# A wait of GpSimd's gathers on VectorE's products of hats in a deformable sampler

## The chip, the cores and the metric

The kernel runs on one core of a Trainium2 chip. The metric is the device time of one execution in microseconds, as the median of several runs. Profiles come from one further execution that the hardware profiler recorded.

## What is computed

Four layers follow one another on eight images of 64 channels and 32 by 32 pixels: a wavelet layer with sparse attention, a layer of convolutions and "adder" convolutions, a layer of quantised convolutions, and a modulated deformable convolution. The change lies in the code of the last two, which the kernel calls the sampler. What matters there of the reference:

```python
def deform_sample(x, py, px):              # x: (8, 64, 32, 32), two groups of 32 channels
    y0, x0 = jnp.floor(py), jnp.floor(px)
    fy, fx = py - y0, px - x0
    ...
    val = corner(y0i, x0i, (1 - fy) * (1 - fx)) + corner(y0i, x0i + 1, (1 - fy) * fx) \
        + corner(y0i + 1, x0i, fy * (1 - fx)) + corner(y0i + 1, x0i + 1, fy * fx)
    return val.reshape(Bb, DG, Cg, K, Hh, Ww)
off_out = conv2d(x, off_w) + off_b[None, :, None, None]
mask = jax.nn.sigmoid(off_out[:, 2 * DG * K:]).reshape(Bb, DG, K, Hh, Ww)
g = deform_sample(x, py, px) * mask[:, :, None]
out = jnp.einsum('odck,bdckhw->bohw', wr, g)
```

For each pixel, each of the two channel groups and each of the nine taps, four neighbouring pixels at a computed place are read and weighed.

## The kernel before, in words

The eight images lie in two halves of four; one "image" of the sampler is a pair, one of each half, on 128 partitions. There are NB = 4 such images and 16 steps in each (STEPS), so 64 steps (NT).

Seven of the nine taps are done by **gathers**. GpSimd (L1959 to L1975) issues, for each step, GK = 14 indirect DMAs; each fetches for 128 pixels one row of 128 floats, the four neighbours of 32 channels, from a table in HBM. They go into one of four buffers (RING = 4, the tile `sampler_G`), so the gathers of step `th` wait for the semaphore `used` to tell that VectorE is done with step `th - 4` (L1970). At an image's first step they also wait for the indices (`indexed`) and for the table (`stored`).

The other two taps are done **densely**: a pixel's weight on each row and each column is a hat function, and VectorE multiplies hats in y with hats in x (the *products of hats*, `mix`, L2055 to L2065; two parts of 128 x 2048 each, after each of which it raises `mixed`). So `mixed` stands at 2 * (n + 1) when step n is done.

In each step the engines do this, each in this order:

- VectorE: `sample(n)` (L2027 to L2039) waits for the 14 gathers of the step (`arrived`), multiplies them with their weights (L2032), adds the four neighbours (L2036), raises `val` and then `used`; then a piece of the next image's preparation (`next_stage`); then `mix(n)`, which waits for ScalarE's hats (`hy`), PE's spread hats in x (`hx_ps`) and PE's use of the products of the step before (`added`).
- PE: `turn_values(n)` transposes the sampled values (L2156); `contract(n - 1)` multiplies the products of hats with the image (L2195); a piece of the next image's preparation, a convolution (L1744) in ten of an image's sixteen steps; `spread_y(n + 1)` and `spread_x(n + 1)` (L2139, L2148), the latter after `mixed` tells that the products of step n are done; `deform(n - 2)`.
- ScalarE: copies the transposed values (L2239) and the dense values (L2268) out of PSUM, does its piece of preparation, and makes the hats of step n + 1 (L2260, L2262).

The preparation of the next image has twelve pieces (STAGES): two pieces of quantising, convolutions, and at last the offsets, from which VectorE makes the next image's gather indices (L1852 to L1872) and weights. PE does piece i in step i, VectorE and ScalarE in step i + 1. The last image has no next one.

The order on each engine is the order of the code; nothing reorders it. All waits are on semaphores.

Of the kernel before, what the change touches and what calls it, by code (L numbers as in the profile page):

```python
# [41 lines left out]
GK = DG * NTAP  # L42
# [150 lines left out]
def program(nc, A, C, out):  # L193
# [3 lines left out]
    with outer:  # L197
# [1462 lines left out]
        def sampler(st, sb, sem):  # L1660
# [50 lines left out]
            sig, x4_ps, x4, s4_ps, hxm, py_ps, hx_ps, hy, mixed, added, v_sb = (  # L1711
                sem(n) for n in ("sig", "x4_ps", "x4", "s4_ps", "hxm", "py_ps", "hx_ps", "hy", "mixed", "added", "v_sb"))
# [245 lines left out]
            with nc.Block() as blk:  # L1958
                @blk.gpsimd  # L1959
                def _(g):  # L1960
                    g.memset(AP[:, :, :], 0.0)
                    g.memset(WB[2][:, :, :], 0.0)
                    g.memset(zeros, 0.0)
                    g.drain().then_inc(cleared, 1)
                    for th in range(NB * STEPS):
                        b, step = th // STEPS, th % STEPS
                        if step == 0:
                            g.wait_ge(indexed, b + 1)
                            g.wait_ge(stored[b], 16 * NSTORE)
                        if th >= RING:  # L1970
                            g.wait_ge(used, th - RING + 1)
                        for k in range(GK):
                            g.indirect_dma_start(G[th % RING][:, k, :], None, tables[b],  # L1973
                                                 bass.IndirectOffsetOnAxis(ap=IDX[:, b % 2, step, k:k + 1], axis=0))\
                             .then_inc(arrived[th % RING], 16)  # L1975
# [134 lines left out]
                def _(t):  # L2110
                    def prepare_x(g):

                        b, k, ti, _, _ = unit(4 * g)
                        if g:
                            t.wait_ge(hxm, g)
                        if g >= 4 and g % 2 == 0:
                            t.wait_ge(e_sb, g // 2 - 1)
                        for e in range(4):
                            mm = t.matmul(MISC[32 * e:32 * e + 32, :], column(channel(e // DG, e % DG, ti) + 1, 32),
                                          half(OFF[:, b % 2], k), start=True, stop=True)  # L2120
                        mm.then_inc(x4_ps, 1)

                    def prepare_mask(g):

                        b, k, ti, _, _ = unit(4 * g)
                        t.wait_ge(sig, b + 1)
                        t.wait_ge(x4, g + 1)
                        for e in range(4):
                            ch = 64 * (e // DG) + 2 * DG * TAPS + (e % DG) * TAPS + NTAP + ti
                            mm = t.matmul(MISC[32 * e:32 * e + 32, :], column(ch, 32), half(SIG[:, b % 2], k),  # L2130
                                          start=True, stop=True)
                        mm.then_inc(s4_ps, 1)
# [193 lines left out]
```

## Time and profile before

| what | value |
|---|---|
| time, median of 3 runs (lowest to highest) | 4012.67 us (4010.67 to 4012.89) |
| span of the profiled execution | 4500.8 us |
| PE busy | 3405.0 us, 76% |
| VectorE (DVE) busy | 3169.4 us, 70% |
| ScalarE (ACT) busy | 2843.2 us, 63% |
| GpSimd (POOL) busy | 907.3 us, 20% |
| software DMA (the gathers) | 28672 packets, 58.78 MB |

The profiled execution's own time is known by its span alone, from the first to the last instruction. It is 488 us longer than the median of the timed runs. Busy times count an engine's instructions without its waits. PE's matmul ends are modelled, so a matmul can end later than its record says; what waits for it shows that. "remote" in a row is a wait whose end the profile could not put down to a known instruction.

### The profile page before, as it was taken

What the parts mean: (1) busy time and instruction counts of PE and PEld (TensorE: products, weight loads), DVE (VectorE), ACT (ScalarE), POOL (GpSimd) and SP (SyncE); (2) the same over time, 40 slices, a digit from 0 to 9 for tenths busy, and PEclk for the clock granted to TensorE, in tenths of its full rate; (3) what the DMA queues carried; (4) which work ended last, traced back from release to release, by engine and by line L of the source; (5) the groups of instructions that cost most, each with busy time, mean ns of one, the idle gap of its engine ahead of it and who ended that gap; (6) DMA issues with size and microseconds to landing.
All of it is one profiled execution on the core that took longest, in us unless ns stands there. A gap on an engine that the chain in (4) does not pass through costs nothing. (4 is left out here: it accounts for less than half of the span.)

```text
span 4500.8 us, 58636 instructions
## 1 busy us (share of the span) xinstructions
PE 3405.0 (76%) x22186; PEld 1347.4 (30%) x22186; DVE 3169.4 (70%) x3652; ACT 2843.2 (63%) x2698; POOL 907.3 (20%) x974
## 2 busy tenths in 40 slices
PE   3777559999999999999999998447556655674445
PEld 2454333233333333333334343112112212221111
DVE  5999768999999984999999994234435444444445
ACT  1444326999999994999999992234434444443444
POOL 2000010000000000000000000445554554545452
PEclk7656569999999999999999998757767777776667
DMA  2200000000000000000000000211211111121110
GB/s 43 89 1 1 1 3 1 1 1 1 1 1 2 2 1 1 1 1 1 1 1 2 2 1 13 52 34 38 54 41 38 47 46 33 43 54 39 39 41 21
DMA packets 117631, 89.65 MB, mean 20 GB/s; under 512 B 96496, under 2 KB 98576, under 8 KB 117340
## 3 DMA queue, kind: packets, MB, share of 16 engines
q0 software_dynamic: 28672, 58.78, 4.7%
q1 hardware_dynamic: 87036, 26.32, 2.6%
q8 instruction: 197, 3.23, 0.3%
q10 hardware_dynamic: 1632, 0.56, 0.1%
q14 instruction: 94, 0.77, 0.1%
HBM read 65.61 MB, written 19.96 MB: 19 GB/s over the span
## 5 line engine op out<-in xcount | busy, mean ns | idle before, releaser
L1556 ACT ACTIVATE adder_layer_Z<-adder_layer_CP,AN 128x2048 f32 x984 | 1873.3, 2013 | 33.4 <-PE PS L1517 32.6
L1517 PE MATMUL PS<-adder_layer_Z,c_adder_out 128*32 128x512 f32 x16896 | 1845.0, 593 | 57.9 <-ACT adder_layer_Z L1556 33.1
L1602 DVE TENSOR_SCALAR adder_layer_Z<-adder_layer_CP,AW 128x2048 f32 x1128 | 1369.9, 1281 | 45.5 <-PE PS L1517 31.5
L1517 PEld LDWEIGHTS PS<-adder_layer_Z,c_adder_out 128*32 128x32 f32 x16896 | 649.6, 110 | 1253.0 <-issue 1176.1
L1973 POOL DMA_INDIRECT sampler_G<-neighbours,sampler_IDX x896 | 849.6, 948 | 834.9 <-DVEq L2039 436.9
L2260 ACT ACTIVATE sampler_HY<-PS,G_hat 128x512 f32<-128x512 f32 x512 | 309.0, 686 | 319.6 <-PE PS L2139 119.6
L1609 DVE SCALAR_TENSOR_TENSOR adder_layer_Z<-adder_layer_CP,AW,adder_layer_Z 128x1024 f32<-128x1024 f32 x384 | 476.4, 1282 | 35.6 <-issue 35.6
L2148 PE MATMUL PS<-sampler_HXM,G_spread 32*128 32x512 f32 x128 | 99.1, 864 | 387.4 <-DVEq L2065 341.9
L2063 DVE TENSOR_TENSOR P<-sampler_HY,PS 128x2048 f32<-128x2048 f32 x64 | 146.4, 2287 | 338.9 <-remote 255.3
L2262 ACT ACTIVATE sampler_HY<-sampler_HY 128x2048 f32<-128x2048 f32 x128 | 244.6, 1911 | 8.7
L1474 POOL MEMSET XP<- 128x4624 f32 x1 | 4.0, 3952 | 1046.4 <-PE PS L1533 1046.4
L1469 POOL MEMSET adder_layer_CP<- 128x4624 f32 x2 | 7.9, 3954 | 1020.3 <-POOLq L1464 1020.2
L2036 DVE TENSOR_REDUCE sampler_VAL<-sampler_G 128x448 f32<-128x1792 f32 x64 | 208.9, 3265 | 5.8 <-issue 0.9
L1744 PE MATMUL PS<-XP,WB 128*128 128x512 f32 x288 | 154.2, 685 | 76.3 <-ACT sampler_HT L1799 52.2
L2063 DVE TENSOR_TENSOR RAW<-sampler_HY,PS 128x2048 f32<-128x2048 f32 x64 | 146.4, 2287 | 87.7 <-remote 65.1
L2024 DVE TENSOR_TENSOR sampler_HXM<-P,PS 128x512 f32<-128x512 f32 x16 | 11.0, 689 | 274.5 <-remote 169.6
L2148 PEld LDWEIGHTS PS<-sampler_HXM,G_spread 32*128 32x128 f32 x128 | 24.8, 241 | 444.9 <-issue 441.7
L2032 DVE TENSOR_TENSOR sampler_G<-sampler_G,PS 128x1792 f32<-128x1792 f32 x64 | 129.3, 2021 | 40.3 <-DMA sampler_G<-neighbours,sampler_IDX 28.7
L2268 ACT ACTIVATE sampler_VD<-PS 128x512 f32<-128x512 f32 x32 | 19.0, 593 | 209.8 <-remote 177.4
L2239 ACT ACTIVATE sampler_VT<-PS 128x384 f32<-128x384 f32 x64 | 31.1, 486 | 184.8 <-remote 145.1
L811 DVE MAX8 top_k_best<-top_k_WK 128x8 f32<-128x256 f32 x384 | 135.1, 415 | 10.3 <-issue 0.5
L699 PE MATMUL PS<-VT,top_k_PT 128*128 128x9 f32 x512 | 102.6, 339 | 50.8 <-ACT top_k_PT L764 50.8
(376 smaller groups left out, 3018.8 us busy)
## 6 DMA issues: line engine op xcount, KB each, us to landing
sampler_G<-neighbours,sampler_IDX POOLq DMA_INDIRECT x896
neighbours<-top_k_zero SPq DMA_DIRECT2D x16, 578.0 KB, 7.2
neighbours<-sampler_HT SPq DMA_DIRECT2D x256, 32.0 KB, 1.7
X<-in_x SPq DMA_DIRECT2D x8, 256.0 KB, 6.3
out<-X SPq DMA_DIRECT2D x8, 256.0 KB
P<-in_L_conv_conv_w SPq DMA_DIRECT2D x4, 144.0 KB
P<-in_L_conv_add_w SPq DMA_DIRECT2D x4, 144.0 KB
RAW<-in_L_conv_w SPq DMA_DIRECT2D x4, 144.0 KB
```

Source lines behind the costliest of these rows:

```text
L811: v.max(best[:, g % 2, u, 8 * r + 1:8 * r + 9], WK[:, u, :])
L1517: mm = t.matmul(PS[32 * j:32 * j + 32, k, :], K["adder_out"][:, 32 * i:32 * i + 32], Z[:, r % SLOTS, j, c:c + BANK], start=False, stop=Fal ...
L1556: op = a.activation(z(r, j), seen(ch, ty, tx), ACT.Relu, bias=ANf[:, weight(ty, tx, j, i)])
L1602: op = v.tensor_scalar(z(r, j), seen(ch, ty, taps[0]), AWf[:, weight(ty, taps[0], j, i)], 0.0, ALU.subtract, ALU.max)
L1609: op = v.scalar_tensor_tensor(out=z(r, j)[:, b], in0=seen(ch, ty, tx)[:, b], scalar=AWf[:, weight(ty, tx, j, i)], in1=z(r, j)[:, b], op0=A ...
L1744: mm = t.matmul(pre(k), w[:, tap, :], src[:, y:y + 16, x:x + W], start=(tap == 0), stop=(last and tap == TAPS - 1))
L1973: g.indirect_dma_start(G[th % RING][:, k, :], None, tables[b], bass.IndirectOffsetOnAxis(ap=IDX[:, b % 2, step, k:k + 1], axis=0))\
L2032: v.tensor_tensor(g3, g3, WP.unsqueeze(2).broadcast_to([128, GK * 4, CG]), ALU.mult)
L2036: v.tensor_reduce(VAL[:, th % 2, :, :], gt[:, :, :].rearrange("p k (q c) -> p k c q", q=4), AX.X, ALU.add)
L2063: v.tensor_tensor(M[part][:, :, :], HY[:, part], HXB.unsqueeze(1).broadcast_to([128, HATS, BANK]), ALU.mult)
L2260: a.activation(HY[:, part, j, :], PYB, ACT.Abs, bias=GR["hat"][:, c:c + 1])
L2262: a.activation(HY[:, part].rearrange("p c f -> p (c f)"), HY[:, part].rearrange("p c f -> p (c f)"), ACT.Relu, scale=-1.0, bias=1.0)\
```

## The change

In GpSimd's loop over the 14 gathers of a step, a wait is put ahead of the eighth, from step 2 on: until `mixed` stands at 2 * (th - 1), that is, until both products of hats of step th - 2 are done.

```diff
                         for k in range(GK):
+                            if th >= 2 and k == GK // 2:
+                                g.wait_ge(mixed, 2 * (th - 1))
                             g.indirect_dma_start(G[th % RING][:, k, :], None, tables[b],
                                                  bass.IndirectOffsetOnAxis(ap=IDX[:, b % 2, step, k:k + 1], axis=0))\
                              .then_inc(arrived[th % RING], 16)
```

GpSimd's instructions of the sampler, from the first gather on, before (the four buffers are `sampler_G0` to `sampler_G3`, the first image's table is `neighbours0`):

```order
L1973 DMA sampler_G0<-neighbours0,sampler_IDX 128x128 [waits sampler_stored0,sampler_indexed]
L1973 DMA sampler_G0<-neighbours0,sampler_IDX 128x128 x13
L1973 DMA sampler_G1<-neighbours0,sampler_IDX 128x128 x14
L1973 DMA sampler_G2<-neighbours0,sampler_IDX 128x128 x14
L1973 DMA sampler_G3<-neighbours0,sampler_IDX 128x128 x14
L1973 DMA sampler_G0<-neighbours0,sampler_IDX 128x128 [waits sampler_used]
L1973 DMA sampler_G0<-neighbours0,sampler_IDX 128x128 x13
```

The same place of GpSimd's queue after the change:

```order
L1975 DMA sampler_G0<-neighbours0,sampler_IDX 128x128 [waits sampler_stored0,sampler_indexed]
L1975 DMA sampler_G0<-neighbours0,sampler_IDX 128x128 x13
L1975 DMA sampler_G1<-neighbours0,sampler_IDX 128x128 x14
L1975 DMA sampler_G2<-neighbours0,sampler_IDX 128x128 x7
L1975 DMA sampler_G2<-neighbours0,sampler_IDX 128x128 [waits sampler_mixed]
L1975 DMA sampler_G2<-neighbours0,sampler_IDX 128x128 x6
L1975 DMA sampler_G3<-neighbours0,sampler_IDX 128x128 x7
L1975 DMA sampler_G3<-neighbours0,sampler_IDX 128x128 [waits sampler_mixed]
L1975 DMA sampler_G3<-neighbours0,sampler_IDX 128x128 x6
L1975 DMA sampler_G0<-neighbours0,sampler_IDX 128x128 [waits sampler_used]
L1975 DMA sampler_G0<-neighbours0,sampler_IDX 128x128 x6
L1975 DMA sampler_G0<-neighbours0,sampler_IDX 128x128 [waits sampler_mixed]
```

No instruction moved and no gather was added; from the third step on, the eighth gather carries a wait. The other engines' queues read as before but for line numbers, which are two higher from L1973 on.

## Rows read from the trace of the kernel before

**Rows 1.** Table of stretches: from:to, length, busy us (instructions) of each engine, PE's clock, DMA share, GB/s.
```profile
0.00:540.00 540.00, 345.10 (x1303) 233.13 (x1304) 442.34 (x1409) 212.57 (x637) 35.41 (x67) 0.63 0.10 28
540.00:2700.00 2160.00, 2027.01 (x17426) 742.64 (x17427) 1950.17 (x1724) 1907.97 (x1050) 16.08 (x7) 0.97 0.01 1
...
2854.40:4500.80 1646.40, 910.40 (x2990) 321.40 (x2990) 715.82 (x418) 685.03 (x967) 849.58 (x896) 0.71 0.16 41
```

**Rows 2.** Timeline of GpSimd, first and last gather: start, duration, instruction, [idle before].
```profile
2854.41 1.16 POOL L1973 DMA_INDIRECT sampler_G<-neighbours,sampler_IDX  x1 [99.47 <-DMA neighbours<-sampler_HT]
...
4438.52 0.94 POOL L1973 DMA_INDIRECT sampler_G<-neighbours,sampler_IDX  x1 [0.30 <-issue]
```

**Rows 3.** Groups of the sampler's stretch: busy us, mean ns, idle before, who ended it.
```profile
L1973 POOL DMA_INDIRECT sampler_G<-neighbours,sampler_IDX x896 | 849.6, 948 | 834.9 <-DVEq L2039 436.9 <-issue 265.9 <-DMA neighbours<-sampler_HT 99.5
```

**Rows 4.** Waits of the sampler's stretch: total us, times, longest.
```profile
DVE P L2063 <- remote: 255.3, 15, 26.1
```

**Rows 5.** Timeline of two steps, GpSimd, VectorE, PE and ScalarE, in part.
```profile
3541.16 0.94 POOL L1973 DMA_INDIRECT sampler_G<-neighbours,sampler_IDX  x1 [15.70 <-DVEq L2039]
...
3548.49 2.02 DVE L2032 TENSOR_TENSOR sampler_G<-sampler_G,PS 128x1792 f32<-128x1792 f32 x1 [0.19 <-issue]
...
3553.97 0.66 PE L2156 MATMUL PS<-c_ident,sampler_VAL 128*128 128x128 f32 x4 [2.24 <-DVEq L2038]
...
3557.41 0.95 POOL L1973 DMA_INDIRECT sampler_G<-neighbours,sampler_IDX  x1 [0.31 <-issue]
3558.66 0.94 POOL L1973 DMA_INDIRECT sampler_G<-neighbours,sampler_IDX  x1 [0.30 <-issue]
...
3564.47 0.49 ACT L2239 ACTIVATE sampler_VT<-PS 128x384 f32<-128x384 f32 x1 [7.51 <-remote]
...
3574.92 0.94 POOL L1973 DMA_INDIRECT sampler_G<-neighbours,sampler_IDX  x1 [0.30 <-issue]
3579.97 2.29 DVE L2063 TENSOR_TENSOR P<-sampler_HY,PS 128x2048 f32<-128x2048 f32 x1 [26.08 <-remote]
...
3590.64 0.95 POOL L1973 DMA_INDIRECT sampler_G<-neighbours,sampler_IDX  x1 [14.77 <-DVEq L2039]
```

**Rows 6.** Timeline, step 1: its last gather and VectorE's first use of it.
```profile
2888.41 0.95 POOL L1973 DMA_INDIRECT sampler_G<-neighbours,sampler_IDX  x1 [0.30 <-issue]
...
2891.02 2.02 DVE L2032 TENSOR_TENSOR sampler_G<-sampler_G,PS 128x1792 f32<-128x1792 f32 x1 [7.45 <-DMA sampler_G<-neighbours,sampler_IDX]
```

**Rows 7.** Timeline of VectorE, step 62 and the start of the last, after the last gather.
```profile
4460.87 2.02 DVE L2032 TENSOR_TENSOR sampler_G<-sampler_G,PS 128x1792 f32<-128x1792 f32 x1 [0.19 <-issue]
4462.97 3.27 DVE L2036 TENSOR_REDUCE sampler_VAL<-sampler_G 128x448 f32<-128x1792 f32 x1
4468.46 2.29 DVE L2063 TENSOR_TENSOR P<-sampler_HY,PS 128x2048 f32<-128x2048 f32 x1 [2.22 <-PE PS L2195]
4470.94 2.29 DVE L2063 TENSOR_TENSOR RAW<-sampler_HY,PS 128x2048 f32<-128x2048 f32 x1 [0.19 <-issue]
4473.41 2.02 DVE L2032 TENSOR_TENSOR sampler_G<-sampler_G,PS 128x1792 f32<-128x1792 f32 x1 [0.19 <-issue]
```

**Rows 8.** Table of stretches: a plain step, then two convolutions of 18 matmul records each.
```profile
4455.92:4468.46 12.54, 9.35 (x38) 3.32 (x34) 9.87 (x4) 10.02 (x14) 0.00 (x0) 0.73 0.00 1
3443.75:3451.74 7.99, 7.99 (x23) 3.67 (x20) 7.30 (x5) 1.27 (x2) 5.92 (x7) 1.00 0.20 58
3583.48:3594.29 10.81, 10.81 (x19) 4.48 (x19) 6.49 (x3) 0.00 (x0) 2.84 (x3) 0.74 0.44 74
```

**Rows 9.** Timeline of VectorE in step 44, which prepares the fourth image's indices.
```profile
4039.67 3.23 DVE L2036 TENSOR_REDUCE sampler_VAL<-sampler_G 128x448 f32<-128x1792 f32 x1
...
4052.47 0.46 DVE L1852 TENSOR_SCALAR sampler_pos<-sampler_T 128x224 f32<-128x224 f32 x2 [9.58 <-ACTq L1806]
...
4060.43 2.29 DVE L2063 TENSOR_TENSOR P<-sampler_HY,PS 128x2048 f32<-128x2048 f32 x1 [0.21 <-issue]
```

## The prediction

> **What bounds the kernel now.** I began with the page and the table of stretches. The program's first 540 us are a sorting and attention stage, up to 2700 us come the adder layers, and the sampler, which the change touches, issues its first gather at 2854.41 us [rows 1, 2]. In that last stretch of 1646.4 us no engine is full: PE is busy 910.40, GpSimd 849.58, VectorE 715.82 and ScalarE 685.03 us [rows 1]. By shares alone nothing there is a bound; the order in time has to tell.
>
> The list of groups and the waits say who waits: GpSimd's 896 gathers stood 834.9 us idle, 436.9 us of it for VectorE's release of a ring buffer; VectorE in turn stood 255.3 us before its products of hats for something the profile cannot name [rows 3, 4]. The timeline of one pair of steps shows how the two hang together [rows 5]. GpSimd starts at 3541.16, released by the sampling of some step n, and issues 28 gathers, for steps n + 4 and n + 5, every 1.25 us without a gap up to 3575.86. VectorE samples step n + 1 from 3548.49, and then stands 26.08 us, up to 3579.97, four microseconds after the burst. ScalarE too stands 7.51 us for a PE result whose matmuls have ended at 3554.63 by the record. From this burst to the next, at 3590.64, it is 49.5 us for two steps; that pattern, a short step and a long one, fills the stretch.
>
> **But this is not what the timed runs do.** The profiled execution spans 4500.8 us, the timed median is 4012.67 us: 488 us less. Where can they be? Up to 540 us VectorE is busy 442.34 of 540 us; in the adder layers PE is busy 2027.01 of 2160 us; both together leave 231 us of idle time on their fullest engines [rows 1]. So most of the 488 us must go in the sampler, where the nameless stalls are. A floor says how far: first gather at 2854.41 [rows 2], 896 gathers [rows 3] at 1.25 us [rows 5], which is 1120 us, and after the last gather's end 1.7 us of landing (the first steps, where VectorE waited for data: gather ended 2889.36, sampling began 2891.02 [rows 6]) and 27.4 us from the last sampling at 4473.41 to the end of the span [rows 1, 7]; the profiled run issued its last gather at 4438.52 [rows 2], long before that end. Sum 2854.4 + 1120 + 1.7 + 27.4 = 4003.5 us. The timed median lies 9 us above that. So I read the timed kernel as **bound by GpSimd's issue rate in the sampler**, 14 x 1.25 = 17.5 us a step, with almost no pause, and the stalls of the profile as belonging mostly to the profiled execution. A step without stage work needs 12.5 us of the others (sampling at 4460.87, the next at 4473.41 [rows 7]), so they can follow.
>
> The Trainium skill ("NOTIFIC — the notification-queue block", 7.1 Overflow: three behaviours, one of which stalls the engine) says that the block that writes trace records always holds back an engine inside itself rather than lose a record. No row here shows that this happened; it only makes the reading above less strange, and no number hangs on it.
>
> **The change, part by part.** It adds 62 waits (steps 2 to 63) to GpSimd, each ahead of the eighth gather; nothing is removed or moved. Queued behind a wait stand the seven gathers of the half and all later steps; VectorE's sampling waits for them. No other engine's queue changes.
>
> - *A wait that finds its count reached* costs nothing that I can see: the gather at 3558.66 carries the wait for a released buffer and starts 0.30 us after the one before, like those without a wait [rows 5]. 62 x 0 = 0. Upward the bound is one semaphore trip; I take 0.
> - *Does it find it reached?* Call G the end of the last gather of step m, with GpSimd never pausing. Sampling starts at G + 1.7 [rows 6]; from there to the end of the second product is 12.4 us (4460.87 to 4473.23 [rows 7]), so step m is mixed at G + 14.0. The eighth gather of step m + 2 is due at G + 0.30 + 17.5 + 8.75 = G + 26.5. **Slack 12.5 us**: no wait in a plain step. The old rule alone (buffer released at G + 1.7 + 5.4 = G + 7.1, first gather of m + 4 due at G + 52.8) had 45.7 us. The change takes 33 us of lookahead away, which costs nothing unless the others fall behind by over 12.5 us.
> - *Steps with stage work.* The step that prepares the next image's indices (three of them) is the latest. In the row, VectorE's reduction ends at 4042.90 and the product begins at 4060.43, 17.5 us against 2.2 us in a plain step (4466.24 to 4468.46) [rows 7, 9]. 15.3 us more than a plain step is 2.8 us over the slack. Of these 9.58 us are a wait for ScalarE, which was late in that row; with ScalarE less than 3 us earlier there is none. Three times 0 to 2.8 us: 0 to 8.4 us; I take 3, nearer the low end, since part of that lateness is the profile's.
> - *The first steps of the sampler*, where the ring is empty and convolutions of the next image begin: 0 to 5 us, an estimate by the same slack with one late convolution (10.81 instead of 7.99 us [rows 8]) and VectorE's stage work; I take 1.
> - *The data's way.* The second half, 7 x 1.25 + 1.7 = 10.5 us after its release, lands before VectorE asks for it, one plain step of 12.5 us after the products it waited for. So even where the wait does hold GpSimd, sampling of that same step is not late by itself; the lost gather time shows one step later.
>
> Sum: 4012.67 + 0 + 3 + 1 = 4017 us, +0.1%. Ends of these terms: +0 to +13 us. In the profiled execution GpSimd ran three steps ahead of the sampling [rows 5], so there the waits will be real and long; its span can move either way, and the time doesn't rest on it.
>
> **The rivals.**
> 1. *The lost lookahead costs: slower.* In eight steps in a row of an image PE also convolves. A plain step costs it 9.35 us, a convolution 7.99 us at a granted clock of 1.00 and 10.81 us in a stretch at 0.74 [rows 8]: 17.3 or 20.2 us against GpSimd's 17.5. At 20.2 the others fall 2.7 us behind per step, 21 us in eight steps; the old rule's 45.7 us swallow that, the new rule's 12.5 don't: 8.8 us lost, with the index step 11.6, in three images 35 us, so 4048 us. It decides from the point at which PE's convolution step passes GpSimd's by 1.6 us (12.5 over 8). For it: the two numbers are close and [rows 8] have both. Against it: with no stalls PE would be nearly always busy in these steps and, as in the row at clock 1.00, at the upper of its two levels, 2.4 GHz.
> 2. *The stalls are in the timed runs too, and shorter bursts relieve them: faster.* In the profile a pair of steps costs 49.5 us, of which 26.08 us are a stall that ends with the burst [rows 5]. Held at the half step GpSimd can issue at most up to the next unmet count, and then the others are let go. But the total can't fall under GpSimd's own 1120 us: 4003.5 us if the timed runs reach the sampler when the profiled one does, less by as much as they reach it earlier. Of the 231 us idle before it I take 10, so 3993 us. Against it: the timed time leaves 9 us, and a wait can't make the issuer faster.
> The Trainium skill ("Perfetto Trace Analysis", What "DMA-bound" means) would call issue the bound only where the issuer's track is solid with DMA slices. GpSimd's is at 52% here (849.58 of 1646.40 us [rows 1]), so by that rule rival 2's premise holds in the profile. Inside a burst it is solid, and the floor above is why I give that less weight.
> 3. *The wait is always reached:* 4012.7 us. It is the low end of the forecast and counts with it.
>
> **How the numbers follow.** Forecast with rival 3: 0.57. Rival 1: 0.28, between 4021 and 4050. Rival 2: 0.15, mostly between 3975 and 4004; it would gain in weight if the 1.25 us of a gather were partly the recording's, which no row can tell. About 0.2%, 8 us, is what a measurement of this kernel can tell from no change. Predicted 4017 us. The range of 3990 to 4046 us leaves out about half of rival 2 below and a quarter of rival 1 above. Faster 0.15, same 0.57, slower 0.28.
>
> **What would show it.** Right: the same time to a few us. In the profile of the changed kernel GpSimd's gaps of 0.30 us stay, most of its idle time is now ended by VectorE's drain after the products instead of its release after sampling, and gathers run about one step ahead of the sampling instead of three. Wrong: VectorE waiting often for arrived data would show that the 10.5 us don't fit; a timed gain over 9 us would show that the floor, and so my reading of the timed runs, is wrong.

## The result, and the profile after

The changed kernel takes **4017.45 us** (median of 20 runs, 4014.21 to 4021.52) where the kernel before takes 4013.05 (median of 20 runs, 4009.39 to 4015.54): 4.4 us more by the medians. The ratio over all runs is 1.0014, 95% interval 1.0008 to 1.0020, which is 3.2 to 8.0 us. It is a small loss, clear of zero, within the 0.2% for which the prediction said "same", and 0.45 us from the predicted time.

The page of the changed kernel begins with its span and the busy time of each engine, and its chain of work gives a share of the span to each engine:

```profile
span 4018.0 us, 58636 instructions
...
PE 3323.6 (83%) x22186; PEld 1330.0 (33%) x22186; DVE 3170.5 (79%) x3652; ACT 2840.5 (71%) x2698; POOL 908.6 (23%) x974
...
POOL 17%; issue 6%; PE 4%; DVE 2%; ACT 1%; SPq 1%; ACTq 0%; DMA 0%; DVEq 0%; POOLq 0%
```

The span lies right at the timed median, 483 us under the span of the profile of before, and GpSimd with its issue gaps (23% together) is the largest part of the chain. The engines did the same work as before; the stalls of [rows 3 to 5] are gone. The groups of instructions say it line by line (busy us, mean ns | idle before them, and what ended most of it):

```profile
L1975 POOL DMA_INDIRECT sampler_G<-neighbours,sampler_IDX x896 | 851.0, 950 | 379.7 <-issue 271.9
...
L2034 DVE TENSOR_TENSOR sampler_G<-sampler_G,PS 128x1792 f32<-128x1792 f32 x64 | 129.4, 2021 | 163.5 <-DMA sampler_G<-neighbours,sampler_IDX 159.0
...
L2065 DVE TENSOR_TENSOR P<-sampler_HY,PS 128x2048 f32<-128x2048 f32 x64 | 146.4, 2288 | 98.0 <-PE PS L2197 91.1
```

L1975 is the line of [rows 3]: its idle time fell from 834.9 to 379.7 us, and of that 271.9 are the 0.30 us gaps of issue. L2065 is the line of [rows 4]: no wait of it is put down to "remote" any more. VectorE now waits for gathered data (159.0 us), so the others follow GpSimd, not the reverse. The waits of the changed kernel from 2800 us to the end, GpSimd's alone (total us, times, longest), show the price of the new wait:

```profile
POOL sampler_G L1975 <- issue: 271.9, 892, 0.3
POOL sampler_G L1975 <- DMA neighbours<-sampler_HT: 100.2, 1, 100.2
POOL sampler_G L1975 <- DVEq L2067: 7.6, 3, 4.4
```

Of the 62 added waits, 59 found their count reached; three held GpSimd, 7.6 us in all. These are the three, in the timeline of GpSimd (start, duration, instruction, [idle before]):

```profile
3110.77 0.94 POOL L1975 DMA_INDIRECT sampler_G<-neighbours,sampler_IDX  x1 [0.30 <-issue]
3116.15 1.33 POOL L1975 DMA_INDIRECT sampler_G<-neighbours,sampler_IDX  x1 [4.44 <-DVEq L2067]
3117.79 0.94 POOL L1975 DMA_INDIRECT sampler_G<-neighbours,sampler_IDX  x1 [0.30 <-issue]
...
3398.65 1.33 POOL L1975 DMA_INDIRECT sampler_G<-neighbours,sampler_IDX  x1 [1.59 <-DVEq L2067]
...
3681.30 1.33 POOL L1975 DMA_INDIRECT sampler_G<-neighbours,sampler_IDX  x1 [1.59 <-DVEq L2067]
```

They are the eighth gathers of steps 14, 30 and 46, two steps after the steps 12, 28 and 44 that prepare the next image's indices. What released the first one stands in VectorE's timeline, at the end of step 12:

```profile
3102.63 0.53 DVE L1852 TENSOR_SCALAR sampler_pos<-sampler_T 128x224 f32<-128x224 f32 x2 [9.57 <-ACTq L1806]
...
3111.09 2.29 DVE L2065 TENSOR_TENSOR P<-sampler_HY,PS 128x2048 f32<-128x2048 f32 x1 [0.57 <-issue]
3113.57 2.29 DVE L2065 TENSOR_TENSOR RAW<-sampler_HY,PS 128x2048 f32<-128x2048 f32 x1 [0.19 <-issue]
```

The second product ends at 3115.86, and GpSimd starts 0.29 us later. The 9.57 us wait for ScalarE is the same as the 9.58 of [rows 9]; in the steps 28 and 44 of this recording it is 7.51 and 7.76 us.

### The profile page after: what moved, and what is told of

Same layout as the page of the kernel before. It is cut to its first block and busy times, and to the rows that moved or that the text cites. A ratio compares the mean times of both kernels' runs of the same rounds, so it can differ in the third digit from the quotient of the medians.

```text
span 4018.0 us, 58636 instructions
## 1 busy us (share of the span) xinstructions
PE 3323.6 (83%) x22186; PEld 1330.0 (33%) x22186; DVE 3170.5 (79%) x3652; ACT 2840.5 (71%) x2698; POOL 908.6 (23%) x974
## 3 DMA queue, kind: packets, MB, share of 16 engines
q8 instruction: 197, 3.23, 0.3%
## 5 line engine op out<-in xcount | busy, mean ns | idle before, releaser
L1975 POOL DMA_INDIRECT sampler_G<-neighbours,sampler_IDX x896 | 851.0, 950 | 379.7 <-issue 271.9
L2034 DVE TENSOR_TENSOR sampler_G<-sampler_G,PS 128x1792 f32<-128x1792 f32 x64 | 129.4, 2021 | 163.5 <-DMA sampler_G<-neighbours,sampler_IDX 159.0
L2065 DVE TENSOR_TENSOR P<-sampler_HY,PS 128x2048 f32<-128x2048 f32 x64 | 146.4, 2288 | 98.0 <-PE PS L2197 91.1
L2150 PE MATMUL PS<-sampler_HXM,G_spread 32*128 32x512 f32 x128 | 86.8, 763 | 136.9 <-DVEq L2067 135.3
L2158 PE MATMUL PS<-c_ident,sampler_VAL 128*128 128x128 f32 (+1 forms) x256 | 57.1, 363 | 156.7 <-DVEq L2040 156.7
L2065 DVE TENSOR_TENSOR RAW<-sampler_HY,PS 128x2048 f32<-128x2048 f32 x64 | 146.4, 2287 | 17.6 <-issue 10.5
L1744 PE MATMUL PS<-XP,WB 128*128 128x512 f32 x288 | 137.0, 633 | 11.8 <-ACT sampler_HT L1799 8.5
L811 DVE MAX8 top_k_best<-top_k_WK 128x8 f32<-128x256 f32 x384 | 135.1, 414 | 10.3 <-issue 0.5
L749 ACT ACTIVATE top_k_sign<-PS,top_k_nthr 128x256 f32<-128x256 f32 x128 | 58.9, 472 | 108.9 <-DVEq L806 108.9
L739 ACT ACTIVATE top_k_junk<-PS,START 128x256 f32<-128x256 f32 x128 | 58.8, 472 | 94.2 <-PE PS L672 94.2
L699 PEld LDWEIGHTS PS<-VT,top_k_PT 128*128 128x128 f32 x512 | 101.9, 305 | 63.1 <-ACT top_k_PT L764 63.1
```

Of the source, the lines that this page charges most:

```text
L699: mm = t.matmul(PS[:, 6, D1 * u:D1 * u + D1], PT[:, u, 128 * mt:128 * mt + 128], VTf[:, c:c + D1], start=(mt == 0), stop=(mt == 1))
L811: v.max(best[:, g % 2, u, 8 * r + 1:8 * r + 9], WK[:, u, :])
L1744: mm = t.matmul(pre(k), w[:, tap, :], src[:, y:y + 16, x:x + W], start=(tap == 0), stop=(last and tap == TAPS - 1))
L2065: v.tensor_tensor(M[part][:, :, :], HY[:, part], HXB.unsqueeze(1).broadcast_to([128, HATS, BANK]), ALU.mult)
```

## The experiments

Theory A: in a run without stalls GpSimd's issue of 896 gathers sets the sampler's time; a wait whose count is reached costs nothing, and every microsecond that GpSimd is held is added to the time. Theory B, its rival: the stalls of [rows 3 to 5] belong to the kernel, and a wait trades one kind of pause for another.

**The kernel before, recorded again.** No edit.

> The kernel before, unchanged, with a new profile. Theory A: the long stalls in the profile of before (span 4500.8 us) belonged to that one recorded execution, since in the profile of the changed kernel (span 4018.0 us) GpSimd issues just as densely and nothing stalls; then the new span lies at 4010 to 4025 us, with gaps of 0.30 us between gathers and VectorE waiting for arrived data. Theory B: a ring that runs three steps ahead brings the stalls whenever it is recorded, and the new wait took them away; then the span is again 4400 to 4600 us while the time stays at 4013 us.

It took 4010.69 us, ratio 0.9995 (0.9984 to 1.0005). The first line of its page:

```profile
span 4009.7 us, 58636 instructions
```

GpSimd's waits from 2800 us on:

```profile
POOL sampler_G L1973 <- issue: 272.8, 895, 0.3
POOL sampler_G L1973 <- DMA neighbours<-sampler_HT: 100.2, 1, 100.2
```

All 895 gathers after the first start 0.3 us after the one before: one burst from 2857.73 to 3980.39 us. Nothing of the 436.9 us of [rows 3] or the 255.3 us of [rows 4] is left. The table of stretches has the sampler's stage beside [rows 1] (from:to, length, busy us of PE, PEld, VectorE, ScalarE, GpSimd, PE's clock, DMA share, GB/s):

```profile
2857.70:4009.70 1152.00, 835.32 (x2990) 302.99 (x2990) 716.35 (x418) 681.94 (x967) 849.91 (x896) 0.79 0.23 59
```

The work is that of [rows 1] in 1152.0 us instead of 1646.4. So the stalls were of that one execution, and this recording, not the first, is what the changed kernel has to be compared with. Its last gather starts at 3979.45, that of the changed kernel at 3987.28:

```profile
3979.45 0.94 POOL L1973 DMA_INDIRECT sampler_G<-neighbours,sampler_IDX  x1 [0.30 <-issue]
```

```profile
3987.28 0.94 POOL L1975 DMA_INDIRECT sampler_G<-neighbours,sampler_IDX  x1 [0.30 <-issue]
```

7.8 us between the two recordings (both start their first gather at 2857.7), and 8.3 us between the spans. That is three holds beyond the usual 0.30 us (4.14 + 1.29 + 1.29 = 6.7 us) and 0.39 us more for each of the three held gathers (1.33 instead of 0.94 us).

**A wait that is nearly always reached.** The products of step n - 3 instead of n - 2:

```diff
-if th >= 2 and k == GK // 2:
-    g.wait_ge(mixed, 2 * (th - 1))
+if th >= 3 and k == GK // 2:
+    g.wait_ge(mixed, 2 * (th - 2))
```

> The same wait at the same place, but for the products of step n-3 instead of n-2: 61 waits, each due 17.5 us later, so with 30 us of slack in a plain step and more than 17 us at the tightest step of the changed kernel's profile. Theory A (the loss of about 4 us is time in which GpSimd is held at the index steps): no wait holds it, 4013 us, as before. Theory B (each wait costs a little, 4.4 us / 62 = 0.07 us): 4017 us.

4012.90 us, ratio 1.0001 (0.9992 to 1.0010). GpSimd's waits:

```profile
POOL sampler_G L1975 <- issue: 272.5, 894, 0.3
...
POOL sampler_G L1975 <- DVEq L2067: 0.3, 1, 0.3
```

61 waits stand in the queue and none holds it: the one that is put down to VectorE is no longer than the usual gap of 0.30 us. What can't be told from zero is the price of all 61 together, under 4 us by the interval.

**The change without the steps behind the index work.**

```diff
-if th >= 2 and k == GK // 2:
+if th >= 2 and k == GK // 2 and th % STEPS not in (14, 15, 0):
```

> The wait as in the changed kernel but left out in the steps 14, 15 and 0 of each image, the ones that wait for the products of the step that prepares the next image's indices and its neighbours. Theory A: 4013 us, as before, since the profile of the changed kernel shows GpSimd held only in steps 14, 30 and 46 (4.7, 1.9 and 2.4 us). Theory B (a cost of each wait, 51 of 62 are left): 4016.6 us.

4011.93 us, ratio 0.9998 (0.9989 to 1.0007). GpSimd has no wait for the products left in the list:

```profile
POOL sampler_G L1975 <- issue: 272.7, 895, 0.3
```

That is the list of the kernel before. With the wait gone from these steps no loss is left that can be told from zero (at most 2.8 us by the interval): the index steps carry it. The expectation's 4.7, 1.9 and 2.4 us are not what the rows show, which is 4.44, 1.59 and 1.59.

**The wait ahead of the whole step**, due 8.75 us earlier:

```diff
-if th >= 2 and k == GK // 2:
+if th >= 2 and k == 0:
```

> The wait ahead of the first gather of a step instead of the eighth: due 7 x 1.25 = 8.75 us earlier. Theory A (issue bound, slack of 12.5 us in a plain step): 3.7 us of slack are left there, and every late step holds GpSimd: the index steps by 8.4 us more than now, the first convolution steps of an image by 4 to 6 us; 25 to 45 us more than the changed kernel, 4042 to 4062 us. Theory B (the issue is not the bound, the others set the pace): within 8 us of the changed kernel, 4017 us.

4085.98 us, ratio 1.0183 (1.0168 to 1.0199): 73 us more than before, and more than was expected.

```profile
POOL sampler_G L1975 <- issue: 272.2, 867, 1.6
POOL sampler_G L1975 <- DMA neighbours<-sampler_HT: 100.6, 1, 100.6
POOL sampler_G L1975 <- DVEq L2067: 75.5, 28, 10.2
```

Of these 28 waits ten are no longer than the usual gap of 0.30 us; 18 held GpSimd, 67 us beyond that gap, 27 of them behind the three index steps. Six gaps of 1.58 us behind held gathers add nearly 8 us. Held time is lost time again (67 + 8 us held, 73 lost), which is theory A; its count of steps was wrong. A plain step has 11.7 - 8.75 = 3 us of slack left under this rule, and I had thought only of the index steps and a few convolutions. The unbroken recording of the kernel before could have told: in it the products of 31 of the 62 steps come less than 8.75 us ahead of the eighth gather that would wait for them.

**The wait for the products of step n - 1:**

```diff
-if th >= 2 and k == GK // 2:
-    g.wait_ge(mixed, 2 * (th - 1))
+if th >= 1 and k == GK // 2:
+    g.wait_ge(mixed, 2 * th)
```

> The eighth gather of step n waits for the products of step n-1 instead of n-2, so nothing but half a step lies between. Theory A (held time of the issuer is lost time, price by the distance): from the products of a plain step 7 gathers of 1.25 us, 1.6 us to the sampling and 12.4 us to the end of the next products follow one another, 22.8 us a step where 17.5 us were; 63 steps x 5.25 us = 331 us, 4344 us, and more in the steps with convolution and index work, up to 4480 us. GpSimd is held at nearly every step by about 5 us or more. Rival (the data's way hides behind the 12.5 us that VectorE needs anyway, as one sentence of the prediction had it): 4085 to 4150 us, little more than in the run in which the whole step waited for the products of n-2.

4502.93 us, ratio 1.1223 (1.1204 to 1.1242): 490 us more. GpSimd's waits:

```profile
POOL sampler_G L1975 <- DVEq L2067: 508.5, 63, 18.3
```

One row each of GpSimd's and VectorE's timeline, a held half step and its first use:

```profile
4172.38 1.33 POOL L1975 DMA_INDIRECT sampler_G<-neighbours,sampler_IDX  x1 [9.87 <-DVEq L2067]
...
4182.72 2.02 DVE L2034 TENSOR_TENSOR sampler_G<-sampler_G,PS 128x1792 f32<-128x1792 f32 x1 [9.83 <-DMA sampler_G<-neighbours,sampler_IDX]
```

Released at 4172.38, the half step is used at 4182.72: 10.3 us, the data's way of the prediction (10.5). But VectorE stands idle for 9.83 us of it. GpSimd is held at every one of 63 steps, and each engine waits for the other in turn. Less 63 usual gaps of 0.30 us the held 508.5 us are 490, again the loss, and the rival falls. Theory A's own figure, at most 4480 us, was low: the plain steps take about 23.5 us (expected 22.8), but the steps with convolution and index work take up to 35.8 us.

**One gather less per step**, from the fifth step on, in the kernel before:

```diff
-for k in range(GK):
+for k in range(GK if th < RING else GK - 1):
...
-v.wait_ge(arrived[th % RING], 16 * GK * (th // RING + 1))
+v.wait_ge(arrived[th % RING], 16 * (GK + (GK - 1) * (th // RING)))
```

> The kernel before, but from the fifth step on only 13 of the 14 gathers of a step are issued: 60 gathers fewer, the fourteenth tap group keeps the values of an earlier step (left out: that data). Nothing else changes, neither VectorE's sampling nor PE's work. Theory A (the sampler is bound by GpSimd's issue rate, so the time is its count of gathers): 60 x 1.25 = 75 us less, about 3938 us; a little more, up to 3960 us, where a stretch of steps with convolution and index work needs over 16.25 us a step from the other engines and then sets the pace. Theory B (the other engines set the pace and GpSimd only follows): 4005 to 4013 us, and GpSimd's waits for a released buffer grow by what its gathers lose.

3941.42 us, ratio 0.9818 (0.9801 to 0.9834): 71 us less. The group of the gathers in that run:

```profile
L1973 POOL DMA_INDIRECT sampler_G<-neighbours,sampler_IDX x836 | 793.6, 949 | 356.4 <-issue 254.2
```

Two of its waits, one of GpSimd and one of VectorE:

```profile
POOL sampler_G L1973 <- DVEq L1872: 1.8, 1, 1.8
...
DVE sampler_G L2032 <- DMA sampler_G<-neighbours,sampler_IDX: 34.6, 6, 22.6
```

The kernel leaves out these 60 gathers and their data and nothing else, and nearly all of their 75 us came off the time. Of the rest, the recording shows 1.8 us in a wait for the next image's indices, 2.6 us in a later start (first gather at 2860.29 instead of 2857.73) and 1.0 us more from the last gather to the end. This is the direct evidence that issue is the bound. It also shows how near the next one is: VectorE waited for data 138.6 us in 38 steps of the kernel before and only 34.6 us in six steps here, and its sampling trailed the last gather of a step by up to 43.4 us (step 45). With four buffers GpSimd is held once that passes about 43.6 us (3 x 16.25 + 0.3 - 5.4, by the prediction's count for the old rule). In the last step it samples 0.19 us after its own products, no longer behind the data:

```profile
3909.64 2.29 DVE L2063 TENSOR_TENSOR RAW<-sampler_HY,PS 128x2048 f32<-128x2048 f32 x1 [0.19 <-issue]
3912.12 2.02 DVE L2032 TENSOR_TENSOR sampler_G<-sampler_G,PS 128x1792 f32<-128x1792 f32 x1 [0.19 <-issue]
```

## Why the prediction was right, and where it was not

**The bound: right.** The floor of 4003.5 us was 6.2 us under the clean recording (4009.7). The first gather starts at 2857.7 instead of 2854.4 (3.3 us), the burst takes 1122.7 instead of 1120 us (2.7), and the end 0.2 more. Of the rest, 1.7 us lie outside the span (the recorded execution was timed at 4011.45 us) and 1.2 between that execution and the median. So the 9 us between floor and timed median held no pause of the sampler at all. By the Trainium skill ("Perfetto Trace Analysis", What "DMA-bound" means) the issuer's track is solid with DMA slices where its sequencer is the bound; in the clean recording GpSimd is busy 849.91 of 1152.0 us, 74%, with a gap of 0.30 us after each gather. The run with 60 gathers fewer decides: each gather not issued took 71 / 60 = 1.2 us off the time, so the gap counts as issue too.

**The stalls belong to the profiled execution: right.** The kernel before, recorded again, has none, nor has any other recording here. Why that execution had them is open (below).

**A reached wait costs nothing: right**, by the run that waits for step n - 3.

**Slack of a plain step: 11.7 instead of 12.5 us.** In the last steps of the changed kernel sampling starts at 3989.85 and the products end at 4003.13, 13.3 us where [rows 7] gave 12.4. VectorE waits 3.23 us for PE's result there instead of 2.22:

```profile
3989.85 2.02 DVE L2034 TENSOR_TENSOR sampler_G<-sampler_G,PS 128x1792 f32<-128x1792 f32 x1 [4.35 <-DMA sampler_G<-neighbours,sampler_IDX]
3991.95 3.19 DVE L2038 TENSOR_REDUCE sampler_VAL<-sampler_G 128x448 f32<-128x1792 f32 x1
3998.36 2.29 DVE L2065 TENSOR_TENSOR P<-sampler_HY,PS 128x2048 f32<-128x2048 f32 x1 [3.23 <-PE PS L2197]
4000.84 2.29 DVE L2065 TENSOR_TENSOR RAW<-sampler_HY,PS 128x2048 f32<-128x2048 f32 x1 [0.19 <-issue]
```

Sampling follows the last gather's end by 1.5 to 1.6 us, near the 1.7 of [rows 6].

**The index steps: right in place, mis-sized.** Each was to cost 0 to 2.8 us, 3 in all. The recording has 4.14, 1.29 and 1.29 us, 6.7 in all and 7.8 with the longer held gathers; timed it is 4.4 us (3.2 to 8.0). So the term was about half of what the recording shows, and its first hold lies over the stated 2.8 us. I took the low end because I put part of ScalarE's lateness down to the profiled execution; it is there undisturbed (7.5 to 9.57 us). In step 12 sampling also began 2.7 us after the last gather instead of 1.6, and the slack was 11.7 us.

**The first steps: 0 instead of 1 us.** The nearest miss is step 4, whose wait is reached 2.6 us before it is due. That the sum came within 0.45 us is in part luck. This miss makes up for 1 us of the one above. The spans differ by 8.3 us, but the recorded execution of the changed kernel was timed at 4019.76 us, 2.3 us over its median. The interval of 3.2 to 8.0 us can't tell a loss of 4 from one of 7.

**Rival 1 fell.** No convolution step held GpSimd; all three holds are index steps. It needed eight convolution steps in a row at about 20 us. In the clean recording never more than two in a row are so slow: in the first image the samplings of the steps 1, 2, 3 and 4 lie 20.6, 19.5 and 14.1 us apart, and VectorE's lateness behind the last gather of its step, 6.7 us at step 3, is back at 1.6 at step 5. The reason that the prediction gave against this rival was half right: in the 175 us from 2875.2 on, ten steps, PE was busy 134.62 us at a mean granted clock of 0.83, and not nearly always busy at the upper level. That lost lookahead does cost once the slack is used up is shown by the wait half a step earlier (73 us). **Rival 2 fell** with its premise: the stalls aren't in the timed runs.

**What would show it: three sentences were wrong.** The prediction expected the profile's waits to be "real and long" and most of GpSimd's idle time to be ended by VectorE's drain after the products: it is 7.6 of 379.7 us. It expected gathers one step ahead instead of three, but three was a feature of the stalled execution; in undisturbed runs of both kernels VectorE mostly samples as soon as the data is there, and GpSimd is then on average 3.1 (before) or 2.4 gathers (changed) into later steps. For the same reason "VectorE waiting often for arrived data" was no sign against the prediction: VectorE waits so 38 times in the kernel before and 40 times in the changed one, because GpSimd is the bound. All three sentences mixed the stalled profile into a forecast for runs that, by its own argument, have no stalls.

**The data's way was only half argued.** That a held half step "is not late by itself" is true of one isolated hold: in the steps 14, 30 and 46 of the changed kernel the last gather had ended 4.9 to 6.2 us before VectorE sampled. When the slack is gone in every step, the 10.3 us stand in full on the path, as the run with n - 1 showed.

## What to carry to other kernels

Compare the span of a profile with the timed median first: where it is longer by a tenth, the waits in it may be of that one execution, and a floor from the issuer's count and spacing says more than they do. Where one queue issues without pause, a wait put into it costs what the work that it waits for is late against its due time, step by step, and little else (here 0.39 us more for each held gather). So make the list of due times for all steps: the plain step's slack (11.7 us here) decides little, the few latest steps decide everything, and a shift of half a step turned 3 holds into 18.

## What the runs showed of the hardware

One recorded execution of the kernel before took 4500.8 us, and seven others, of this kernel and of close relatives, show no such stalls. In that one the engines waited long after matmuls that had ended by the record: in [rows 5] ScalarE starts at 3564.47 on a result of matmuls that began at 3553.97 and took 0.66 us, some 10 us earlier. The trace's records of semaphore updates place the delay. PE's count for these matmuls rises at 3564.44, 9.8 us after their recorded end, and ScalarE starts at once; the count `added` (PE has used the products of the step before), the last that VectorE waited for in its 26.08 us of [rows 5], rises at 3579.84, and the product starts at 3579.97. So the delay lies ahead of PE's signal and not in the engines that wait for it. In the second recording of the same kernel these counts of PE rise at most 0.06 us after the recorded end of the matmul.

The trace of the stalled execution also lacks records: it holds 12531 semaphore updates where the second recording holds 25506, and of the gathers' own 896 x 16 = 14336 updates it holds 3055 where the second holds 14268. So its waits put down to "remote" say little. No run brought the stalls back, and what held PE's signals back stays open. The Trainium skill ("NOTIFIC — the notification-queue block", 7.1 Overflow: three behaviours, one of which stalls the engine) would allow for it, since it says that the internal pipeline of the block that writes trace records presses back rather than lose a record inside the block, and that its stalls would mean a throttled engine. No run here shows that it was this, and in this trace records are missing all the same.

The same program also shows how sharply the time turns with lookahead: waiting at the half step for the products of n - 3, n - 2 and n - 1 gave 4012.9, 4017.5 and 4502.9 us.
